# A convolution and whitening kernel: the second pass in 64x128 tiles, with the transposed image as stationary operand

## The reference

```python
x = x + conv(groupnorm(x))        # spectral convolution: rfft2, 32x17 modes mixed by head, irfft2, plus bias
x = x + whiten(groupnorm(x))      # 16 groups of 16 columns along w: covariance, Cholesky, inverse

def whiten(x):                    # c is the last axis (w, 256), n = all other elements
    f  = x_flat - mean            # (256, n)
    fg = f.reshape(16, 16, n)
    cov = ((1 - 1e-3) * fg @ fg.T / denom + 1e-3 * eye) / denom
    inv_sqrt = solve_triangular(cholesky(cov), eye, lower=True)
    return inv_sqrt @ fg          # block diagonal over w, blocks of 16
```

## Time and profile before

| | |
|---|---|
| median of 3 runs | 3541.8 us (3539.89 to 3545.57) |
| profiled execution | 3536.93 us, span 3535.0 us |
| PE busy | 2898.4 us, 82% of the span |
| PEld busy | 2038.3 us, 58% |
| DVE busy | 2541.8 us, 72% |
| ACT busy | 1146.3 us, 32% |
| POOL busy | 1116.4 us, 32% |
| bytes moved | 1001.81 MB, mean 283 GB/s |

### The profile page before, as it was taken

One profiled execution on the slowest core, in us unless ns is written; L12 is line 12 of the kernel. 1 busy time (PEld: TensorE's weight loads), 2 busy tenths in 40 slices (PEclk: granted clock), 3 DMA queues, 4 the chain that ended last, 5 costly groups with the idle time before them and its releaser, 6 DMA issues.

```text
span 3535.0 us, 230090 instructions
## 1 busy us (share of the span) xinstructions
PE 2898.4 (82%) x98565; PEld 2038.3 (58%) x98565; DVE 2541.8 (72%) x4358; ACT 1146.3 (32%) x2860; POOL 1116.4 (32%) x1434
## 2 busy tenths in 40 slices
PE   6888888888886342366499999999999999999998
PEld 3555555555554332122377777777777777777776
DVE  4777777777776335755477777777777777777777
ACT  1222222222221221000144444444444444444444
POOL 4666666666665112455111111111111111111111
PEclk8999999999998555799799999999999999999999
DMA  7999999999999761699388888888888888888887
GB/s 229 330 322 331 327 330 323 326 326 327 333 327 274 93 92 19 205 349 352 118 302 302 302 300 301 301 302 300 301 302 301 302 303 300 301 302 302 300 300 279
DMA packets 630257, 1001.81 MB, mean 283 GB/s; under 512 B 103712, under 2 KB 464176, under 8 KB 630192
## 3 DMA queue, kind: packets, MB, share of 16 engines
q1 hardware_dynamic: 528816, 912.44, 78.5%
q10 hardware_dynamic: 101376, 88.39, 8.7%
HBM read 639.40 MB, written 361.28 MB: 283 GB/s over the span
## 4 chain that ended last, share of the span: by engine, by line
PE 50%; issue 15%; ACT 14%; ACTq 10%; DMA 6%; DVE 5%; SPq 0%; DVEq 0%; POOL 0%; POOLq 0%
PE bank L593 15%; ACT reg L645 13%; PE bank L584 11%; ACTq L653 6%; PE bank L421 6%; DMA reg<-xh_d 5%; PE bank L432 5%; PE bank L440 4%; PE bank L454 3%; PE bank L564 2%; PE bank L501 2%; PE bank L525 1%; ACT xh L645 1%; DVE reg L866 1%; PE bank L463 1%
## 5 line engine op out<-in xcount | busy, mean ns | idle before, releaser
L645 ACT ACTIVATE reg<-bank 128x512 f32<-128x512 f32 (+3 forms) x1696 | 844.7, 529 | 1105.7 <-PE bank L593 941.1
L1064 DVE STREAM_TRANSPOSE reg<-bank 128x256 f32<-128x256 f32 x2048 | 738.8, 418 | 335.5 <-PE bank L610 335.5
L768 POOL TENSOR_TENSOR reg<-reg 128x512 f32<-128x512 f32 x512 | 685.9, 1340 | 433.8 <-PE bank L432 402.0
L1068 DVE SCALAR_TENSOR_TENSOR reg<-reg,m,mwhit 128x1024 f32<-128x1024 f32 x512 | 657.8, 1285 | 72.1 <-DVE reg L1064 38.2
L593 PE MATMUL bank<-tab,reg 64*128 64x256 f32 x4096 | 692.5, 404 | 0.0
L822 POOL TENSOR_TENSOR reg<-reg,tab 128x64 f32<-128x64 f32 x512 | 164.2, 321 | 1550.1 <-ACT reg L645 828.0
L854 DVE TENSOR_TENSOR reg<-reg 128x512 f32<-128x512 f32 x512 | 526.5, 1028 | 36.6 <-DVE gmask L872 20.2
L610 PE MATMUL bank<-reg 32*32 32x128 f32 x32768 | 547.0, 279 | 1.7 <-DVE reg L1064 1.7
L610 PEld LDWEIGHTS bank<-reg 32*32 32x32 f32 x32768 | 370.5, 103 | 210.3 <-issue 171.5
L584 PE MATMUL bank<-tab,reg 64*128 64x64 f32 x8704 | 443.5, 235 | 46.2 <-ACT reg L645 46.1
L593 PEld LDWEIGHTS bank<-tab,reg 64*128 64x128 f32 x4096 | 458.5, 187 | 28.0 <-issue 0.7
(11 more groups left out here) (121 smaller groups left out, 1765.2 us busy)
## 6 DMA issues: line engine op xcount, KB each, us to landing
reg<-in_x_dram SPq DMA_DIRECT2D x256, 1024.0 KB, 8.2
reg<-in_x_dram SPq DMA_DIRECT2D x512, 512.0 KB, 3.9
out_dram<-reg SPq DMA_DIRECT2D x512, 512.0 KB, 2.9
xh_d<-xh ACTq DMA_DIRECT2D x128, 512.0 KB
reg<-xh_d SPq DMA_DIRECT2D x128, 512.0 KB, 5.9
gram_d<-gram ACTq DMA_DIRECT2D x64, 256.0 KB
reg<-gram_d SPq DMA_DIRECT2D x64, 256.0 KB, 4.8
spec_d<-psu ACTq DMA_DIRECT2D x512, 8.5 KB
```

What stands on the lines that cost most here:

```text
L645: copy = lambda o, i, **k: nc.scalar.activation(o, i, ACT.Copy, **k)
L768: nc.gpsimd.tensor_tensor(out=halves[:, q % 2, 1], in0=x_in[:, 2 * q:2 * q + 2, 0], in1=x_in[:, 2 * q:2 * q + 2, 1], op=ALU.subtract).then ...
L1064: ins = v.transpose(o_sb[:, q].rearrange("p n (f w) -> p f n w", f=2)[:, :, :, BL * j:BL * j + BL], bank[4 + j][:, 0:W].rearrange("p (f n ...
L1068: v.scalar_tensor_tensor(out=o_sb[:, q], in0=o_sb[:, q], scalar=m1[:, ds(t * 4 + q, 1)], in1=mwhit[:, :].unsqueeze(1).to_broadcast([P, 4, W]),
```

## The change

The 32x32 tiles of the whitening are gone. The transposed image is now the stationary operand (64x128 pieces of `xt_sb`), and the whitening matrix, widened to 64 columns, is the moving one, so the result comes out with rows of the image on the partitions: VectorE adds straight from PSUM, without transposing. Bank 3 is copied by VectorE (`turned_image`), bank 2 by ScalarE. `whitened` is cut into three parts of 4, 4 and 8 products; the first stands behind the first half of the convolution's products, the second behind the second half, the third ahead of the next `turn`. `spectrum_turned` is in two 64-row pieces and stands at the end of its pair.

```diff
-        xt_sb, a = cut(big, a, 2, 2, 2, H)
-        wr, a = cut(big, a, 2, 2, BL)
-        wp, a = cut(big, a, 2, 2, BL)
-        wd, a = cut(big, a, 2, BL)
+        xt_sb, a = cut(big, a, 2, 2, 4, P)
+        wr, a = cut(big, a, 2, 2, KH)
+        wp, a = cut(big, a, 2, 2, KH)
+        wd, a = cut(big, a, 2, KH)
...
-                mm(bank[0][:, W:W + P], cs[:, m].rearrange("p a b -> p (a b)"), T("eye"), start=True, stop=True,
-                   is_transpose=True).then_inc(S["ct_mm"], 1)
+                for c in range(2):
+                    k = slice(KH * c, KH * c + KH)
+                    ins = mm(bank[c][:, W:W + KH], cs[k, m].rearrange("p a b -> p (a b)"), T("eye")[k, k],
+                             start=True, stop=True, is_transpose=c == 1)
+                ins.then_inc(S["ct_mm"], 1)
...
-                pe.wait_ge(*nth("xt2_copied", t * 8 + 2 * q))
+                pe.wait_ge(*nth("xt2_act", t * 4 + q))
+                pe.wait_ge(*nth("xt2_dve", t * 4 + q))
...
+            def convolved(t, q, half):
+
+                if half == 0:
+                    pe.wait_ge(*nth("z_ready", t * 2 + q // 2 + 1))
+                for c in range(2):
+                    k = slice(KH * c, KH * c + KH)
+                    ins = mm(bank[2 + c][:, H * half:H * half + H], z_sb[k, q // 2, q % 2, P * half:P * half + P],
+                             T("hb")[k], start=False, stop=True, skip_group_check=True)
+                    if half == 1:
+                        ins.then_inc(S["xt2_mm"], 1)
...
+            def whitened(t, q, part):
+
                 e = q % 2
-                for half in range(2):
-                    for i in range(4):
-                        for j in range(4):
-                            r = slice(BL * j, BL * j + BL)
-                            ins = mm(bank[4 + j][BL * i:BL * i + BL, P * half:P * half + P],
-                                     wp[r, e, half], xt_sb[r, e, half, i // 2].rearrange(
-                                         "p (n h) -> p n h", h=KH)[:, :, BL * (i % 2):BL * (i % 2) + BL],
-                                     start=half == 0, stop=True, skip_group_check=True)
-                ins.then_inc(S["o_mm"], 1)
+                if part == 0:
+                    pe.wait_ge(*nth("w_ready", t * 4 + q + 1))
+                    pe.wait_ge(*nth("xt2_act", t * 4 + q + 1))
+                    pe.wait_ge(*nth("xt2_dve", t * 4 + q + 1))
+                    pe.wait_ge(*nth("o_ready", t * 4 + q - 1))
+                for r in ((0,), (1,), (2, 3))[part]:
+                    for half in range(2):
+                        for g in range(2):
+                            k = slice(KH * g, KH * g + KH)
+                            at = P * r + KH * half
+                            ins = mm(bank[4 + 2 * e + g][:, at:at + KH], xt_sb[k, e, half, r], wp[k, e, half],
+                                     start=r == 0 and half == 0, stop=True, skip_group_check=True)
+                if part == 2:
+                    ins.then_inc(S["o_mm"], 1)
...
-                    if q % 2 == 0 and ahead:
-                        spectrum_turned(*ahead)
-                    turn(t, q, before)
+                    turn(t, q)
+                    for half in range(2):
+                        convolved(t, q, half)
+                        if before:
+                            whitened(*before, half)
                     if q % 2 == 1 and ahead:
                         widened(*ahead)
                     if before:
-                        whitened(*before)
+                        whitened(*before, 2)
+                    if q % 2 == 0 and ahead:
+                        spectrum_turned(*ahead)
...
+            def turned_image(t, q):
+
+                dve.wait_ge(*nth("o_mm", t * 4 + q - 1))
+                dve.wait_ge(*nth("xt2_mm", t * 8 + 2 * q + 2))
+                v.tensor_copy(xt_sb[:, q % 2, :, :, KH:P], bank[3][:, :].rearrange("p (f r h) -> p f r h", f=2, r=4)
+                              ).then_inc(S["xt2_dve"], 1)
+
             def result(t, q):
                 dve.wait_ge(*nth(f"out_stored{q}", t * 16))
                 dve.wait_ge(*nth("o_mm", t * 4 + q + 1))
-                for j in range(4):
-                    ins = v.transpose(o_sb[:, q].rearrange("p n (f w) -> p f n w", f=2)[:, :, :, BL * j:BL * j + BL],
-                                      bank[4 + j][:, 0:W].rearrange("p (f n h) -> p f n h", f=2, n=4))
-                ins.then_inc(S["o_turned"], 1)
-                dve.wait_ge(*nth("o_turned", t * 4 + q + 1))
-                v.scalar_tensor_tensor(out=o_sb[:, q], in0=o_sb[:, q], scalar=m1[:, ds(t * 4 + q, 1)],
-                                       in1=mwhit[:, :].unsqueeze(1).to_broadcast([P, 4, W]),
-                                       op0=ALU.add, op1=ALU.subtract).then_inc(S["o_ready"], 1)
+                for g in range(2):
+                    by = lambda a: a.rearrange("p r (f g w) -> p (r f) g w", f=2, g=2)[:, :, g]
+                    ins = v.scalar_tensor_tensor(
+                        out=by(o_sb[:, q]), in0=bank[4 + 2 * (q % 2) + g][:, :].rearrange("p (n w) -> p n w", n=8),
+                        scalar=m1[:, ds(t * 4 + q, 1)], in1=by(mwhit), op0=ALU.add, op1=ALU.subtract)
+                ins.then_inc(S["o_ready"], 1)
```

More of the change, by code:

```diff
@@ L226, in whiten_kernel @@
         fac = sb("fac", [M, M])
-        whit, msum, mwhit = sb("whit", [P, 2, P]), sb("msum", [P, 2, P]), sb("mwhit", [P, W])
+        whit, msum = sb("whit", [P, 2, P]), sb("msum", [P, 2, P])
         o_sb, a = cut(reg1, 0, 4, 4, W) if NP >= 256 else cut(sb("o_buf", [P, 4096]), 0, 4, 4, W)
@@ L233, in whiten_kernel @@
         z_sb, a = cut(big, a, 2, 2, W)
-        xt_sb, a = cut(big, a, 2, 2, 2, H)
-        wr, a = cut(big, a, 2, 2, BL)
-        wp, a = cut(big, a, 2, 2, BL)
-        wd, a = cut(big, a, 2, BL)
+        xt_sb, a = cut(big, a, 2, 2, 4, P)
+        wr, a = cut(big, a, 2, 2, KH)
+        wp, a = cut(big, a, 2, 2, KH)
+        wd, a = cut(big, a, 2, KH)
         cs, a = cut(big, a, 2, 2, KH)
+        mwhit, a = cut(big, a, 4, W)
         names = """tab_in beta_in beta_zero
@@ L558, in _, with strips @@
             pe.wait_ge(*nth("mw_ready", 1))
+            def strips(a, half):
+                return a.rearrange("p (g f w) -> p g f w", g=2, f=2)[:, :, half]
             def spectrum_turned(t, m):
@@ L573, in widened, with turn @@
                 ins.then_inc(S["z_mm"], 1)
-            def turn(t, q, before=None):
+            def turn(t, q):
                 pe.wait_ge(*nth(f"x_re_in{q}", t * 16 + 16))
-                pe.wait_ge(*nth("xt2_copied", t * 8 + 2 * q))
+                pe.wait_ge(*nth("xt2_act", t * 4 + q))
+                pe.wait_ge(*nth("xt2_dve", t * 4 + q))
                 for half in range(2):
@@ L584, in turn @@
                             ins = mm(bank[2 + c][:, at:at + KH], x_re[k, q, r, P * half:P * half + P], T("eye")[k, k],
-                                     start=half == 0 and r == 0, stop=False, is_transpose=half + r + c > 0, skip_group_check=True)
+                                     start=half == 0 and r == 0, stop=False, is_transpose=half + r + c > 0,
+                                     skip_group_check=True)
                 ins.then_inc(S[f"x_re_used{q}"], 1)
-                pe.wait_ge(*nth("z_ready", t * 2 + q // 2 + 1))
@@ L634, in _ @@
             four(NP // 4 - 1, last=True)
-            may_whiten(NP // 4 - 1, 3)
-            whitened(NP // 4 - 1, 3)
+            for part in range(3):
+                whitened(NP // 4 - 1, 3, part)
         def root(act, n, a):
@@ L710, in _ @@
             act.wait_ge(*nth("mw_mm", 1))
-            copy(mwhit[:, :], bank[4][:, 0:W], scale=1.0 / ROWS).then_inc(S["mw_ready"], 1)
-            for j in range(4):
-                r = slice(BL * j, BL * j + BL)
-                ins = copy(wd[r], whit[r, :, BL * j:BL * j + BL])
+            for r in range(4):
+                ins = copy(mwhit[:, r], bank[4][:, 0:W], scale=1.0 / ROWS)
+            ins.then_inc(S["mw_ready"], 1)
+            for g in range(2):
+                k = slice(KH * g, KH * g + KH)
+                ins = copy(wd[k], whit[k, :, KH * g:KH * g + KH])
             ins.then_inc(S["wd_ready"], 1)
@@ L726, in turned_kept @@
                 act.wait_ge(*nth("z_mm", t * 2 + m - 1))
-                copy(ct_sb[:, m], bank[0][:, W:W + P]).then_inc(S["ct_ready"], 1)
+                copy(ct_sb[:, m].rearrange("p (c k) -> p c k", c=2), low[:, :, W:W + KH]).then_inc(S["ct_ready"], 1)
             def widened_kept(t, m):
@@ L737, in four @@
                     act.wait_ge(*nth("o_mm", t * 4 + q - 1))
[L738 to L741, removed]
+                    act.wait_ge(*nth("xt2_mm", t * 8 + 2 * q + 1))
+                    copy(xt_sb[:, q % 2, :, :, 0:KH], bank[2][:, :].rearrange("p (f r h) -> p f r h", f=2, r=4)
+                         ).then_inc(S["xt2_act"], 1)
+                    if q % 2 == 1 and not (last and q >= 2):
```

(17 more changed lines are left out.)

19 lines of the change are left out of this document (7 added, 12 removed).

## The result

The changed kernel takes 3613.03 us (median of 4 runs, 3604.58 to 3620.19) against 3540.85 us for the kernel before: a ratio of 1.0201, with a 95% interval from 1.0177 to 1.0226. It is 72 us slower; the forecast was 61 slower, 3603 us.

What follows compares the result with a forecast made beforehand. TensorE's order was taken to bound the kernel, DMA some way behind. Its terms summed to 3.60 us a pair against 3.48, +61 us over 512 pairs on 3541.8, so 3603 us; eight-in-ten range 3370 to 3700 us.

Steps and rivals of the forecast that it cites:

- TensorE bounds, DMA is behind: Second pass: TensorE's order sets the 3.48 us a pair; DMA would need 3.00 us a pair at 349 GB/s.
- The whitening's 16 slots at 0.11: Whitening: each slot is the larger of its stream and the next load, 16 x 0.11 = 1.76 us a pair.
- The other terms: Rest of TensorE's pair: `turn` and convolution 1.51 us, `widened` 0.22, `spectrum_turned` 0.11.
- The skill's rule on row groups: Whitening: by the rule load and stream add, raising the sum 0.86 us a pair; the forecast did not follow it.
- Sum, 3.60 us a pair: TensorE's work in the changed kernel: 1.51 + 1.76 + 0.22 + 0.11 = 3.60 us a pair against 3.48.
- The four stretches: Two pairs split at convolution ends: behind even +0.53 us, behind odd +0.04, odd convolution -0.34; +0.23, or 0.12 a pair.
- Costed at nothing: VectorE's bank 3 copy (0.71 us) and additions, larger `scaled` and `wp`, copy of z, queue order: no time added.
- Loads at 0.10 us: Rival, whitening loads: 16 slots are 1.60 us, a pair 3.44, time 3522 us; chance 0.10.
- Hidden loads: Rival: convolution slots take in whitening loads placed between them, -0.44 us a pair, 3378 us; chance 0.09.
- Cheap loads: Rival: whitening loads no dearer than the transposes', about 0.06 us a record; DMA then bounds, 3296 us; chance 0.09.
- New waits: Rival: `turn` waits for both engines' copies, whitening for `w_ready` and `o_ready`; 0.2 us a pair, 3706 us; chance 0.12.
- Adding up: Rival: load and stream add, one set of weights a row group; 4.46 us a pair, 4044 us; chance 0.05.

Runs made afterwards that it cites:

- The shortened kernel: The changed kernel without a quarter of the whitening's products (12 a pair instead of 16): 3398.7 us, ratio 0.9611 to the kernel before.
- doubled stream: The changed kernel with each whitening product streaming 128 columns of the whitening matrix instead of 64, same loads: 3611.81 us, 1.0227 times the kernel before.
- narrower loads: The changed kernel with 96 instead of 128 columns in each stationary piece of the whitening, same count of products: 3435.88 us, ratio 0.9714.
- the two reorderings: The kernel before with spectrum_turned in two pieces at the even pair's end and ScalarE's copy of z ahead of scaled: 3522.17 us, ratio 0.995.
- the placement experiment: The changed kernel with all whitening parts behind the convolution's products instead of between them: 3621.09 us, ratio 1.0245 to the kernel before.
- The combination: The kernel before with spectrum_turned split at the even pair's end, copy of z ahead of scaled, and the odd-pair transposes' wait behind the convolution: 3452.67 us, 0.9767.
- the run with one small tile: The changed kernel with one extra product in a 32x32 tile in each pair: 3799.46 us, ratio 1.0743 to the kernel before.

## Why the prediction was right

- **TensorE bounds, DMA is behind.** Right: PE 1400.00 of 1400 us, DMA share 0.81 (0.82 forecast). The shortened kernel shows the order of the two: with a quarter of the slots gone it is faster, DMA stands at 0.93, and PE still has next to no idle time.
- **The whitening's 16 slots at 0.11.** This term decided the sign. The loads of the changed kernel follow each other by 0.112 us, so it is 1.79 us instead of 1.76. These 0.03 us are the difference between the pace measured, 3.63, and the 3.60 of the sum; over 512 pairs they are 15 us, where the forecast missed the time by 10. The other terms, 1.84 us in all, fit what is left of 3.63. That a slot is the load and not the stream is shown by the doubled stream (no change) and by the narrower loads (177 us less).
- **The skill's rule on row groups.** The Trainium skill, page "TensorE: Matmul & The Clock Gate", Part 3, says that a load overlaps products in flight only when the row group differs; by this the sum would have been 0.86 us a pair higher. The doubled stream settles it for f32 products of this shape: the load of the same row group does overlap the stream in flight, and the measurement decides. (The section "The mechanism" of that Part also lets a load go ahead when it targets a background weight buffer, and with that the measurement agrees.)
- **Sum, 3.60 us a pair.** Measured 3.63.
- **The four stretches.** The total stood, but their reading did not: "0.33 before the 32x32 tiles and 0.34 for VectorE's transposes go" puts both down as prices of the kernel before. The first is one (0.37 us a pair with its way back). The second was not by itself: removed alone it gave nothing, and with the two reorderings 65 to 70 us. In the sum this did no harm, since the new pair was counted whole and not as the old pair less its waits.
- **Costed at nothing.** Right: PE has no wait of note. VectorE's copy took 692 ns (0.71 forecast), an addition 746 (0.71), 2.18 us a pair for the copy and two additions.
- **Rivals.** Loads at 0.10 us: they stand 0.112 apart. Hidden loads: refuted by the placement experiment. Cheap loads: 188 ns each and not 0.06 apart, refuted. New waits: none of PE in the rows. Adding up: refuted.

What the comparison with the kernel before hides is that it holds two changes. The combination above keeps the 32x32 tiles, has reorderings like those of the change, and stands at 0.9767; the changed kernel stands at 1.0201. So against a kernel in that order the new whitening, with the copies that belong to it, costs 154 us, twice what the comparison shows.

The Trainium skill, page "TensorEngine Tiling (Array Packing)", Key Properties, says that a change of tiling mode drains the engine; the run with one small tile agrees, 0.37 us a pair. The gain from leaving the small tiles was real and was in the change, but the loads cost more than it gave.

## What to carry to other kernels

Count loads, not columns streamed, when choosing which f32 operand is stationary. In the 64x128 tiles measured here a record of a row group takes the larger of its stream and the next load, so a wide stationary operand under a narrow moving one is paid at the load's rate, and the placement between longer products doesn't change that. Two waits that stand in parallel can each be worth little until both are gone (here 0 us for the one, 14 for the other, about 80 together); test them together before writing one off. When a large rewrite carries small reorderings with it, try those alone: here they and one moved wait, on the old kernel, gave 0.9767, while the rewrite that they came with gave 1.0201.

## What the hardware showed

- Streaming 128 columns instead of 64 behind each load of 128 columns was free in f32, to within the intervals (1.0227 against 1.0201). The slot theory had expected it.
- One product of 32 columns in a tile of another size cost 0.37 us a pair, more than three of the whitening's slots (0.4 to 0.6 was expected).
- Loads of 96 columns took 161 ns against 188, 27 ns for 32 columns, 0.84 ns a column; the estimate from two other lines had been 0.78.
